# Selective scan in one block: steps, row spreading and recurrence side by side, D on TensorE, a quarter of the C products on GpSimd

## The reference, cut to what matters

```python
        def selective_scan(u, delta, A, Bm, Cm, D):
            dA = jnp.exp(delta[..., None] * A)
            dBu = delta[..., None] * Bm[:, :, None, :] * u[..., None]

            def step(h, xs):
                dA_t, dBu_t, C_t = xs
                h = dA_t * h + dBu_t
                y = jnp.einsum('bdn,bn->bd', h, C_t)
                return (h, y)
            Bsz, L, Din, N = dA.shape
            h0 = jnp.zeros((Bsz, Din, N), dtype=u.dtype)
            _, ys = lax.scan(step, h0, (jnp.moveaxis(dA, 1, 0), jnp.moveaxis(dBu, 1, 0), jnp.moveaxis(Cm, 1, 0)))
            y = jnp.moveaxis(ys, 0, 1)
            return y + u * D
```

## Time and profile before

| | us |
|---|---|
| median of three runs | 4396.85 |
| lowest and highest run | 4392.42, 4407.57 |
| the profiled execution | 4394.22 |
| its span in the trace | 4392.5 |
| PE, DVE, ACT, POOL busy | 3877.4, 2997.9, 2355.4, 1695.3 |
| scan_inputs in the trace | 1515.1 to 1591.5 |
| scan_steps | 1591.8 to 1645.9 |
| scan_states | 1646.1 to 1902.5 |

### The profile page before, as it was taken

How to read it: one execution, slowest core, us unless ns; L and a number is a source line. 1 busy time by engine, 2 the same in 40 slices (tenths; PEclk the granted TensorE clock), 3 DMA queues, 4 the chain that set the end, 5 groups by cost and what they waited for, 6 DMA issues and landing times. The chain is left out here.

```text
span 4392.5 us, 50969 instructions
## 1 busy us (share of the span) xinstructions
PE 3877.4 (88%) x17656; PEld 2209.3 (50%) x17656; DVE 2997.9 (68%) x3608; ACT 2355.4 (54%) x3611; POOL 1695.3 (39%) x1007
## 2 busy tenths in 40 slices
PE   7996899999999685668999779999999979769997
PEld 6884344444444261137788534444444425347885
DVE  4333877878787359954888667777777734477886
ACT  2221477777777533312777426666566641247775
POOL 0001487787778606510000126666556650000000
PEclk9997899999999878889999869999999999779998
DMA  9997566676666400021888646666666550407886
GB/s 317 329 339 263 168 155 156 154 155 149 154 152 145 120 5 10 0 80 41 331 323 325 239 127 154 154 144 152 139 153 151 122 132 1 107 31 295 323 327 242
DMA packets 301737, 753.52 MB, mean 172 GB/s; under 512 B 55854, under 2 KB 89390, under 8 KB 267946
## 3 DMA queue, kind: packets, MB, share of 16 engines
q1 hardware_dynamic: 245322, 562.03, 38.7%
q0 software_dynamic: 47456, 171.46, 19.5%
q10 hardware_dynamic: 8704, 16.78, 1.1%
HBM read 485.01 MB, written 99.42 MB: 133 GB/s over the span
## 5 line engine op out<-in xcount | busy, mean ns | idle before, releaser
L776 ACT ACTIVATE prob<-psum 128x512 f32<-128x512 f32 x1552 | 891.4, 595 | 437.1 <-PE psum L676 399.0
L951 POOL TENSOR_TENSOR den_pool<-den_pool,prob 128x1024 f32<-128x1024 f32 x372 | 938.8, 2524 | 228.6 <-DVE den_pool L863 196.8
L676 PE MATMUL psum<-q_stack,k_ring 98*128 98x512 f32 x2048 | 1006.1, 509 | 20.4 <-ACT prob L776 14.5
L651 PE MATMUL psum<-k_ring,q_stack 96*128 96x512 f32 x2048 | 693.1, 423 | 106.1 <-DVE row_max L834 36.4
L830 DVE TENSOR_REDUCE row_max<-psum 128x1 f32<-128x1024 f32 x512 | 616.0, 1220 | 243.7 <-PE psum L651 240.6
L834 DVE CUSTOM_DVE_ANT_0 psum<-psum,mask_q 128x1024 f32<-128x1024 f32 x512 | 627.1, 1233 | 202.9 <-PE psum L651 187.8
L676 PEld LDWEIGHTS psum<-q_stack,k_ring 98*128 98x128 f32 x2048 | 395.3, 194 | 621.8 <-ACT prob L776 272.4
L1928 DVE TENSOR_TENSOR weight_lo<-weight_raw,weight_hi 128x2048 fp32r<-128x2048 f32 x240 | 548.0, 2289 | 132.6 <-ACT weight_hi L1871 131.5
L694 PE MATMUL psum<-prob,x 128*32 128x512 f32 x3104 | 517.5, 613 | 0.9 <-ACT prob L776 0.9
L651 PEld LDWEIGHTS psum<-k_ring,q_stack 96*128 96x128 f32 x2048 | 395.2, 200 | 213.5 <-issue 84.5
L1871 ACT ACTIVATE weight_hi<-weight_raw 128x2048 fp32r<-128x2048 f32 x240 | 457.7, 1917 | 69.9 <-DMA weight_raw<-in_L_ffn_w 35.5
(11 more groups left out here) (428 smaller groups left out, 6351.0 us busy)
## 6 DMA issues: line engine op xcount, KB each, us to landing
weight_raw<-in_L_ffn_w SPq DMA_DIRECT2D x120, 1024.0 KB, 6.9
den_dma<-prob POOLq DMA_DIRECT2D x204, 512.0 KB, 5.0
k_ring<-k_hi SPq DMA_DIRECT2D x1024, 64.0 KB, 2.3
weight_raw<-in_L_ffn_Wu SPq DMA_DIRECT2D x60, 1024.0 KB, 7.2
weight_raw<-in_L_ffn_Wd SPq DMA_DIRECT2D x60, 1024.0 KB, 5.8
den_dma<-xnT POOLq DMA_DIRECT2D x68, 512.0 KB, 4.9
k_ring<-k_lo SPq DMA_DIRECT2D x512, 64.0 KB, 2.6
ctxT<-in_ctxT SPq DMA_DIRECT2D x16, 1024.0 KB, 9.6
```

Of the source, the lines that this page charges most:

```text
L651: ins = e.matmul(max_banks(q)[:, a * KC:(a + 1) * KC], q_stack[h % n_q][0:QROWS, i * P:(i + 1) * P], k_ring[0:QROWS, (n + a) % kring, :], ...
L676: e.matmul(k.bank(b % 2), k_ring[:, n % kring, kt * P:(kt + 1) * P], q_stack[h % n_q][:], start=not masked, stop=True, skip_group_check=ma ...
L776: e.activation(prob[b // 2 % n_p][:, b % 2, :], k.bank(b % 2), ACT.Exp, scale=scale).then_inc(s_exp, 1)
L951: e.tensor_tensor(den[:], den[:], tile, ALU.add).then_inc(s_dpool, 1)
```

## The change

scan_steps is gone. Its loads, the product with x_proj and the selector move into scan_inputs; all else goes into one block with the recurrence.

- PE, behind the last projection, multiplies with x_proj group by group as u gets its Silu.
- ACT: A, then D_diag (D on the diagonal of eight 128 x 128 tiles), then Abs and Exp per group straight from PSUM, Ln for group 0 and for the rest, the first two decays, and then one decay per state with the copies of late rows in between. DVE keeps max(x, 0) as delta.
- Rows are spread in the order SPREAD: B 0 to 7 (copied by DVE), then C 0, B 8, C 1, B 9 up to C 7, B 15, then C 8 to 15 (copied by ACT), with two banks, 2 and 7. Two rows ahead of the sum of state n, PE spreads the rows for n + 2.
- DVE makes delta and du for groups 0 and 1, GpSimd for groups 2 to 7, one group after each fourth step.
- States 2, 6, 10 and 14 of each group: the scan writes its states over its inputs in the SBUF tile db, and GpSimd multiplies with C two steps later. The other twelve are as before. Decays have two PSUM banks instead of three.
- D u enters y as a first matmul with D_diag; the gate is one product, behind the tenth scan instead of the sixth.

The diff, cut to what is spoken of:

```diff
...
+                for dst, src in ((w_steps.xp, k.i["L0_attn_x_proj_w"].rearrange("(k p) n -> p k n", p=P)),
+                                 (w_steps.dtw, k.i["L0_attn_dt_proj_w"]), (w_steps.dtb, k.i["L0_attn_dt_proj_bC"]),
+                                 (w_steps.dcol, k.i["L0_attn_DC"]),
+                                 (w_steps.a, k.i["L0_attn_A_log"].rearrange("(k p) n -> p k n", p=P))):
+                    e.dma_start(dst[:], src).then_inc(s_steps, 16)
                 k.clear_old(e)
+                e.wait_ge(s_steps, 80)
...
+                rows = sel.shape[0]
+                e.tensor_copy(sel[:], k.ident[0:rows, DTR:rows].unsqueeze(2).to_broadcast([rows, 2 * NST, P]))
...
+                e.wait_ge(s_steps, 80)
+                for m in range(GT):
+                    e.wait_ge(s_u, m + 1)
+                    e.matmul(k.bank(7)[0:DTR + 2 * NST, :], w_steps.xp[:, m, :], u[:, m, :], start=m == 0,
+                             stop=m == GT - 1)
...
+POOL_C = (2, 6, 10, 14)
+
+EARLY = 8
+SPREAD = ([("B", st) for st in range(EARLY)] +
+          [row for st in range(EARLY) for row in (("C", st), ("B", EARLY + st))] +
+          [("C", st) for st in range(EARLY, NST)])
...
-    n_da, n_h, n_db = 3, 3, 4
+    n_da, n_h, n_db = 2, 3, 4
...
-            return k.bank(n_da + n % n_h)
+            return db_of(n) if n in by_pool else k.bank(3 + by_dve.index(n) % n_h)
 
         def y(m):
-            return k.bank(n_da + n_h + m % 2)
+            return k.bank(6 + m % 2)
+
+        def spread_bank(j):
+            return k.bank((2, 7)[j % 2])
...
+                def copy_row(j):
+                    n, st = SPREAD[j]
+                    e.wait_ge(s_sel, j + 1)
+                    e.activation(spread[n][:, st, :], spread_bank(j), ACT.Copy).then_inc(s_late, 1)
+
+                def decays(n):
+                    m, st = divmod(n, NST)
+                    if n == 0:
+                        e.wait_ge(s_a, 2)
+                        e.wait_ge(s_relu, GT)
+                    if st == 0 and m < 2:
+                        e.wait_ge(s_delta, m + 1)
+                    elif st == 0:
+                        e.wait_ge(s_pdelta, m - 1)
                     if n >= n_da:
                         e.wait_ge(s_h, n - n_da + 1)
-                    m, st = divmod(n, NST)
                     e.activation(da(n), delta[:, m, :], ACT.Exp, scale=a[:, m, st:st + 1]).then_inc(s_da, 1)
+
+                e.activation(a[:], a[:], ACT.Exp).then_inc(s_a, 1)
+                for m in range(GT):
+                    e.activation(d_diag[:, m, :], k.ident[:], ACT.Copy, scale=w.dcol[:, m:m + 1]).then_inc(s_diag, 1)
+                for m in range(GT):
+                    e.wait_ge(s_dtmm, m + 1)
+                    e.activation(du[:, m, :], k.bank(m % 3), ACT.Abs, bias=w.dtb[:, m:m + 1]).then_inc(s_abs, 1)
+                    e.wait_ge(s_abs, m + 1)
+                    e.activation(du[:, m, :], du[:, m, :], ACT.Exp, scale=-1.0).then_inc(s_expabs, 1)
+                e.wait_ge(s_expabs, GT)
+                e.activation(du[:, 0, :], du[:, 0, :], ACT.Ln, bias=1.0).then_inc(s_ln, 1)
+                e.activation(du[:, 1:, :], du[:, 1:, :], ACT.Ln, bias=1.0).then_inc(s_ln, 1)
+                for n in range(n_da):
+                    decays(n)
+                for n in range(last):
+                    for row in (("C", n), ("B", n + EARLY)):
+                        if row in SPREAD:
+                            copy_row(SPREAD.index(row))
+                    if n + n_da < last:
+                        decays(n + n_da)
...
+                def steps(m):
+
+                    e.wait_ge(s_ln, 2)
+                    e.wait_ge(s_relu, m + 1)
+                    e.tensor_tensor(delta[:, m, :], delta[:, m, :], du[:, m, :], ALU.add).then_inc(s_pdelta, 1)
+                    e.wait_ge(s_pdelta, m - 1)
+                    e.tensor_tensor(du[:, m, :], delta[:, m, :], u[:, m, :], ALU.mult).then_inc(s_pdu, 1)
...
+                    if m == 0 and NH * (g + 1) <= EARLY:
+                        e.wait_ge(s_early, NH * (g + 1))
+                    elif m == 0:
+                        e.wait_ge(s_late, late(("B", NH * (g + 1) - 1)))
                     e.tensor_tensor(db[step % n_db][:], du[:, m, :].unsqueeze(1).to_broadcast([P, NH, T]),
-                                    bc[0][:, g * NH:(g + 1) * NH, :], ALU.mult).then_inc(s_db, 1)
+                                    spread["B"][:, g * NH:(g + 1) * NH, :], ALU.mult).then_inc(s_db, 1)
+
+                def c_states(n):
+                    if n < NST:
+                        e.wait_ge(s_late, late(("C", n)))
+                    e.wait_ge(s_h, n + 1)
+                    e.tensor_tensor(db_of(n), db_of(n), spread["C"][:, n % NST, :], ALU.mult).then_inc(s_cp, 1)
+
+                for step in range(GT * per + 2):
+                    if step < GT * per:
+                        inputs(step)
+                    for n in range(NH * (step - 2), NH * (step - 1)):
+                        if n in by_pool:
+                            c_states(n)
+                    if step % per == 1 and 2 <= step // per + 2 < GT:
+                        steps(step // per + 2)
...
-                    e.scalar_tensor_tensor(out=u[:, m, :], in0=u[:, m, :], scalar=dcol[:, m:m + 1], in1=y(m),
-                                           op0=ALU.mult, op1=ALU.add).then_inc(s_y, 1)
-                    e.wait_ge(s_y, m + 1)
-                    e.tensor_tensor(zs[:, m, :], zs[:, m, :], u[:, m, :], ALU.mult).then_inc(s_z, 1)
+                    e.tensor_tensor(zs[:, m, :], zs[:, m, :], y(m), ALU.mult).then_inc(s_z, 1)
...
+                for m in range(GT):
+                    e.wait_ge(s_abs, m + 1)
+                    e.tensor_scalar(delta[:, m, :], k.bank(m % 3), w.dtb[:, m:m + 1], 0.0, ALU.add, ALU.max
+                                    ).then_inc(s_relu, 1)
+                for j in range(EARLY - 2):
+                    copy_row(j)
+                e.wait_ge(s_relu, GT)
+                steps(0)
+                for j in range(EARLY - 2, EARLY):
+                    copy_row(j)
+                steps(1)
...
-                    if n > 0:
+                    if n > 0 and n - 1 in by_dve:
                         c_states(n - 1)
                     m, st = divmod(n, NST)
-                    if st == 5 and m > 0:
+                    if st == 9 and m > 0:
...
+                def rows_of(st):
+                    for row in (("C", st), ("B", st + EARLY)):
+                        if row in SPREAD:
+                            spread_row(SPREAD.index(row))
...
+                for j in range(EARLY):
+                    spread_row(j)
+                rows_of(0)
+                rows_of(1)
                 for n in range(last):
                     m, st = divmod(n, NST)
-                    if st == 0 and m >= 2:
-                        e.wait_ge(s_y, m - 1)
-                    e.wait_ge(s_c, n + 1)
-                    e.matmul(y(m), k.ident[:], db_of(n), start=st == 0, stop=st == NST - 1).then_inc(s_sum, 1)
+                    if n + 2 < NST:
+                        rows_of(n + 2)
+                    if st == 0:
+                        if m == 1:
+                            e.wait_ge(s_late, len(SPREAD) - EARLY)
+                        if m >= 2:
+                            e.wait_ge(s_z, m - 1)
+                        e.wait_ge(s_diag, m + 1)
+                        e.matmul(y(m), d_diag[:, m, :], u[:, m, :], start=True, stop=False)
+                    e.wait_ge(*c_done(n))
+                    e.matmul(y(m), k.ident[:], db_of(n), start=False, stop=st == NST - 1).then_inc(s_sum, 1)
...
```

More of the change, by code:

```diff
@@ L1312, in _ @@
             def _(e):
-                for n in range(last):
+                def copy_row(j):
[11 more added lines that the diff above has]
+                        e.wait_ge(s_pdelta, m - 1)
@@ L1319, in _, with inputs @@
             @block.gpsimd
             def _(e):
-                for step in range(GT * per):
+                def steps(m):
[4 more added lines that the diff above has]
+                    e.tensor_tensor(du[:, m, :], delta[:, m, :], u[:, m, :], ALU.mult).then_inc(s_pdu, 1)
+                def inputs(step):
@@ L1374, in l0_scan @@
         zs = k.sbuf(outer, "z_silu", [P, GT, T], F32)
[L1375 removed]
         with ExitStack() as ctx:
[L1377 to L1383 removed]
+            w_steps = StepWeights(k, ctx)
+            sel = k.sbuf(ctx, "row_select", [DTR + 2 * NST, 2 * NST, P], F32R)
+            scan_inputs(k, u, zs, w_steps, sel)
+            scan_states(k, ctx, u, zs, w_steps, sel, s_half)
         with ExitStack() as ctx:
```

168 lines of the change are left out of this document (73 added, 95 removed).

## The result

| us | before | changed |
|---|---|---|
| median (runs) | 4396.48 (6) | 4369.14 (6) |
| lowest, highest run | 4385.21, 4407.57 | 4358.60, 4376.06 |
| profiled execution, its span | 4394.22, 4392.5 | 4374.73, 4372.7 |
| start of scan_inputs to copy of dbc | 91.5 | 82.5 |
| copy of dbc to first scan | 44.2 | 32.5 |

The changed kernel takes 0.9936 of the time before, 95% interval 0.9917 to 0.9955: 27 us less, not the 49 of the forecast. The stretch that the change touches is 34.7 us shorter, and the rest of the program, whose code is the same, 14.9 us longer in this execution.

A forecast was written before the change was run, and what follows sets the result against it. DVE was taken to bound the recurrence. Terms -9.8 - 11.9 - 44.7 + 17.3 = -49.1 us took the profiled 4394.22 to 4345.1, median 4348; 8-in-10 range 4336 to 4362.

The forecast's parts named there:

- Part 1: Start of the block, up to dbc's copy: x_proj directly behind the last projection, dbc copied at 1596.7; -9.8 us.
- Part 2: From dbc's copy to the first scan: 32.3 us instead of 44.2, 5.6 of them port lock; -11.9 us.
- Part 3: Recurrence at steady pace: fewer DVE products with C and shorter gates, 207.1 us instead of 251.8; -44.7 us.
- The rival that turns the sign: Recurrence: 32 in-place scans each wait 2 to 3.2 us for GpSimd; +64 to +102 us, 4412 to 4450; chance 0.04.
- the first rival's first half: Recurrence: GpSimd becomes the bound, its products taking 1.7 us; +11 us, 4359; chance 0.19 for the whole rival.
- The first rival's second half: First group: PE's clock stays low throughout; +8 us, 4356; chance 0.19 for the whole rival.
- Part 4: First group, rows still being spread: three gaps of 12.9 us together plus clock loss after gaps; +17.3 us.
- The gaps: First group: three DVE waits of 3.1, 5.1 and 4.7 us, from rows queued behind sums and GpSimd's inputs.
- some 2.2 us for each gap: First group: cost of PE's clock being at 0.50 for a while after each idle gap.
- The upper end of +25: First group with the clock low throughout: 3.4 us per state for six states, 2.6 after; +25 instead of +17.3.

The follow-up runs named there:

- e4: Changed kernel with group 1's delta and delta_u made by GpSimd instead of DVE; median 4361.4 us.
- e3: Changed kernel with each B or C row spread by two matmuls of 128 rows (selector of 0.5) instead of 64; 4358.6 us.
- e2: Changed kernel with hi and lo parts stacked, each B or C row spread by one 128-row matmul instead of two of 64; median 4352.0 us.
- e5_again: Changed kernel with GpSimd's product with C ahead of its next inputs, run a second time; 4337.9 to 4355.1 us (first time 4345.6 to 4368.5).
- e1_group0_dve: Changed kernel with all 16 of the first group's products with C on DVE, none on GpSimd; 4332.8 us.
- e10_order_full: Changed kernel with GpSimd's products with C ahead of its inputs and rows spread by two 128-row matmuls; median 4344.8 us.

## Why the prediction was wrong

By its steps, for the profiled execution (4345.1 forecast, 4374.7 measured, 29.6 apart):

- **Part 1**, right: -9.8 forecast, -9.0 measured from the stage's start. That dbc is copied at 1595.6 (forecast 1596.7) owes 1.9 us to a stage that started earlier in this trace.
- **Part 2**, right: 32.3 forecast, 32.5 measured, with the two waits for the port where they were placed: each of group 1's steps stands behind one of GpSimd's inputs. e4 measures them: 5.3 us (forecast 5.6). By the Trainium skill, "SBUF — State Buffer", "SBUF: two separate sides", such an instruction waits for the lock's holder; the trace agrees (4.06 and 4.87 us).
- **Part 3**, right: no wait of DVE in the steady groups. The gates bring 25.6 (251.8 - 226.2; forecast 25.5), the products with C 0.63 us each or somewhat more (0.592). The rival that turns the sign, scans held up by GpSimd, is dead: 1212 ns. GpSimd at 1265 ns keeps up, so the first rival's first half fell too.
- **The first rival's second half**, PE low through the first group, is what came. It had been given +8 us and took 14.0.
- **Part 4 failed.** 17.3 forecast, 31.3 measured: 14.0 of the 29.6. The gaps and their reasons were as written, and e3 comes to the same sum where the assumption holds (17.8). That it comes so close is in part luck: "some 2.2 us for each gap" stands in the sum twice and not for all three gaps, which would give 19.5. The assumption was that the clock comes back a few us after each gap, by the earlier trace rows, where PE had nothing but sums. The row that spoke against it was there, spreading alone at 0.50 throughout, and I used it for the start only. With rows of 64 in the mix the clock did not come back in this kernel until they were all spread, and with rows of 128 it did. The upper end of +25 was too low as well: it took 3.4 and 2.6 us per state at the low clock, while the trace has 4.01 and 3.15 (1668.91 to 1672.06).
- **The rest of the program**, 14.9 of the 29.6, was taken as unchanged. It is, in code: 15 traces of twelve kernels give 3967.3 to 3984.3 us for it. Before's is among the lowest, and the changed kernel's two are the highest. Where the 14.9 us lie is seen by cutting both traces at the same places of the program. One piece, around l1_linear, takes 152.5 us in the changed kernel (first row) and 142 before (second), with the same work and a clock of 0.84 against 0.92. Another, ahead of it, takes 1094.5 us against 1088 at 0.95 in both; no cause is shown for that.

```profile
3567.50:3720.00 152.50, 129.81 (x560) 78.31 (x560) 79.50 (x117) 27.18 (x44) 8.41 (x12) 0.84 0.16 41
```

```profile
3598.00:3740.00 142.00, 119.63 (x560) 70.25 (x560) 79.50 (x115) 27.07 (x44) 8.09 (x12) 0.92 0.17 42
```

In sum: the stretch was forecast at 423.9 - 49.1 = 374.8 us and took 389.2, 14.4 more (14.0 from part 4, 0.8 from part 1, 0.2 from part 2, less 0.6 between the last gate and the experts); the rest adds 14.9 and what lies around the span 0.3. The medians are 21 us off: 14 from part 4, and some 7 from the rest of the program, of which I can't say how much is chance. The range ended at 4362; with part 4's real size the centre would have been 4362, and a range that took in the rest's spread would have held 4369.

## What to carry to other kernels

A wait of PE that is counted as an idle gap can also cost the clock afterwards, and whether the clock comes back depends on what PE then does: look in the trace for a stretch with the same mix of matmuls, not for one that is merely busy. Two half-height matmuls that add up in PSUM are better stacked into one full one (e2: 17.3 us less). Where a queue holds work that others need at once (GpSimd's product) behind work that itself waits (its inputs), swap them; and when a stage's gain is to be told from a total, measure how far the untouched rest moves.

## What the runs showed of the hardware

- PE stayed at 1.2 GHz through 40 us of unbroken matmuls (e5_again, 1632 to 1672), and through 21 us in the changed kernel, with selector matmuls on 64 rows in the mix, and through 25 us with nothing else (the kernel before, 1618 to 1643). With the same matmuls on 128 rows it was back at 2.4 GHz within 5 to 6 us each time (e3_two_full). Once it was up, it stayed up with 64 rows in the mix (e1_group0_dve, 1.00 for 28 us). The Trainium skill, "TensorE: Matmul & The Clock Gate", "Part 1: The HAM clock gate", has the clock released by activity and calls the moment variable between runs; the runs agree that it varies (e5 has it in some executions and not in others), but in these rows PE's busy time alone did not release it, and the measurement decides.
- A state with four selector matmuls on 64 rows between sums on 128 rows costs PE more than one with 128 rows throughout. At the high clock it takes 2.18 us (e1_group0_dve) against 1.78 (e10_order_full), 0.40 us for two changes of height; at the low clock 4.01 (the changed kernel, 1644.02 to 1648.03) against 3.58 (e3_two_full, 1650.31 to 1653.89). The two at the high clock, in order of time on PE; first e1_group0_dve, then e10_order_full:

```profile
1641.31 1.13 PE L1471 MATMUL psum<-dB_u,ident 128*128 128x512 f32 x2
1642.37 0.49 PE L103 MATMUL psum<-dbc_hi,row_select 64*128 64x512 f32 x1
...
1643.49 1.12 PE L1471 MATMUL psum<-dB_u,ident 128*128 128x512 f32 x2
```

```profile
1641.71 1.02 PE L1477 MATMUL psum<-dB_u,ident 128*128 128x512 f32 x2
1642.17 1.49 PE L103 MATMUL psum<-dbc_hi_lo,row_select 128*128 128x512 f32 x4
1643.49 1.02 PE L1477 MATMUL psum<-dB_u,ident 128*128 128x512 f32 x2
```

The Trainium skill, "TensorEngine Tiling (Array Packing)", "Key Properties", says that a change of tiling mode drains TensorE; these rows fit it, though no run here isolates it.
